# First attention of a four-layer kernel: constants loaded in order of use, later chunks' modulation and projections placed between heads

## The chip, the cores and the metric

The kernel runs on one core of a Trainium2 chip. The metric is the device time of one launch in microseconds (us), median of three runs. The core has five engines with a queue each, which work in the order of their queues and meet through semaphores: TensorE (PE; its weight loads are listed apart as PEld), VectorE (DVE), ScalarE (ACT), GpSimd (POOL) and SyncE (SP), which issues the loads here.

## What is computed

`x` has 16 samples of 128 tokens with 128 features, `cond_8` has 8 numbers a sample. Four layers follow, each `x = x + attention(condition(x))` and `x = x + ffn(condition2(x))`. The change touches the condition and the attention of layer 0 and the weights of its condition2:

```
# L0 condition: a linear layer plus low-rank parts, weighted by cond_8
y = x @ W_base.T + b_base + 2 * sum_e cond_8[:, e] * ((x @ As[e].T) @ Bs[e].T)
# L0 attention: 16 heads of 8 features; q, k and v are scaled by the cosine and the
# sine of a learned phase times an amplitude; softmax; output projection Wo
x = x + attention(y)
# L0 condition2: each sample has its own weight, a blend of 8 masked matrices
y = x @ (sum_g cond_8[:, g] * (weight[g] * mask)).T + bias
# L0 ffn: weights rounded to 4 bits in blocks of 32, activations to 16 bits with one
# scale for the whole tensor (a maximum over everything), so nothing passes it early
# layers 1 to 3: route tokens or samples by the two largest of 8 (top 2 of cond_8)
```

All tensors are 32-bit floats. The sample-wise weights come from `cond_8` alone, and so do the two largest experts of each sample (M8, IDX, WW), which the layers behind use.

## The kernel before

A program in Python writes one list, `order`, of steps (kind and operands); then each engine walks the same list and issues its own part of each step. So the order of the list is the order in every queue. `in_order` (line 64) makes the list from items: an item is a list of stages. In each round it takes one new item and does one stage of it and one stage of each item still alive, the newest first. Semaphore waits stand ahead of the instruction that needs them, and everything later in that queue waits too. Buffers come from rings: `take` gives the next free slot with the signals it must wait for, `give` returns it. For products there are four PSUM banks in ring RA, two in RB and two in RC.

The 16 samples are four chunks (n = 0 to 3) of four, 512 columns. The parts at issue:

- *Loads* (L1398, SP's queue): `cst` (the constants of the first stage, 844.5 KB), `x` in four parts of 256 KB, `l0b` (second projection weights), `w8` (eight matrices), `cst2`, `b2`, `fw` (ffn weights), `l1c`. TensorE and VectorE wait for `cst` and `x` before their first work, ScalarE and POOL for `cst`.
- *Modulation* of a chunk (`cond_items`, line 260): VectorE scales the low-rank matrices (L1995), TensorE multiplies (L1456), VectorE adds the base weight (L1999), TensorE applies the result to x (L1463), ScalarE evicts into Y (L1780). Chunk 0 is done at once, with `prep2` inside: the angle of the phases in six VectorE steps (L2002 to L1976), Sin on ScalarE (L1773), MOD (L2014), then the maxima (L2018) and indices (L2022) of cond_8 for later layers, and their mix with an Exp (L1775). Chunks 1 to 3 are items ahead of the attention.
- *Projection* of a chunk (`proj` in `mh_attn`): TensorE makes q and k with two products each (L1474, L1475) and v with four (L1482). VectorE shifts Y for v (L2041, L2042), turns q and k (stt, L1979) and spreads v (L2055).
- *Heads*: a chunk has 8 items ("heads" here, each one of 4 samples and one half of the 16 heads): scores (L1499), maxima and subtraction (L2075, L2078), exponent (L1792, L1795), turns (L1433, L1434 and the evictions L1800), values and sums (L1515, L1519), for the second half also the normalisation (L2085, L2087), at the end of a chunk the output product (L1526) and the sum into X (L2090). For each j of the four samples POOL makes masked copies of k (`kb`, L2551, four instructions of 128x256), one half item ahead.
- *Beside the heads*: from the fourth entry of the list on each takes up to two small steps: 33 of `wbot_steps` (the mask, L2094, then 4 x 8 blends: VectorE does one sample of four, L2100 or L1979, POOL the other three, each by a multiply (L2561) and an add (L2566)) and 20 of `ffn_weights` (L2109 to L2121, and turns L1531). Behind the last head stands `cond2` (L1540), which reads the blended weights.

Items run in this order: modulation of chunks 1 to 3, projection 0, projection 1, the heads of chunk 0, and projection n+1 in the middle of the heads of chunk n.

Of the kernel before, what the change touches and what calls it, by code (L numbers as in the profile page):

```python
# [15 lines left out]
NB = 16  # L16
S = 128
NC = 4
# [72 lines left out]
CONST = [("ident", 128), ("condT", 16), ("hm4", 4), ("mask", 128), ("sumw", 128),  # L91
# [11 lines left out]
CF = CL["maskT"][0]  # L103
# [34 lines left out]
def build(nc, xT, cst, l0b, w8, b2, fw, fd, l1c, moe1, l1f, moe2, moe3, l2f, moe4, l3f, xs, ys, out):  # L138
    with ExitStack() as ctx:
# [72 lines left out]
        def step(kind, **at):  # L212
# [13 lines left out]
            "cst": [(CC[:, 0:CF], cst[:, 0:CF])], "l0b": [(A1[:, 256:512], l0b)], "x": XIN, "w8": [(A0[:, 12800:13824], w8)],  # L226
# [16 lines left out]
        for name in ("cst", "x", "l0b", "w8", "cst2", "b2", "fw", "l1c"):  # L243
            load(name)
# [15 lines left out]
        def cond_items(key, i, src_key):  # L260
            items = []
            for n in range(NC):
                st = {}

                def s0(n=n, st=st):
                    at = step("cw", i=i, n=n, g=SG.take())
                    at["scaled"] = tick("cond_vec")
                    at["pa"] = RA.take()
                    at["mm"] = tick("cond_mm")
                    SG.give(at["g"], at["mm"])  # L270
                    at["w"] = st["w"] = SG.take()
                    at["sum"] = st["sum"] = tick("cond_vec")
                    RA.give(at["pa"], at["sum"])

# [11 lines left out]
        def mh_attn(i, in_key, out_key):  # L286
# [23 lines left out]
            for n in range(NC):  # L310
                st = chunk[n] = {}

                def proj(n=n, st=st):
                    if n == 0:
                        at = step("zeros", aps=[s.ap for s in RV.slots], after=[] if i == 0 else [sig["l2f_last"]])
# [3 lines left out]
                    if i == 0:  # L319
                        at["shift"] = tick("att_vec")  # L320
                    for x in "qk":
                        at["p" + x], at["r" + x] = RA.take(), RB.take()
                        at["mm" + x] = tick("att_mm")
                        if i == 3:
                            at["rot" + x] = tick("att_vec")
# [5 lines left out]
                    RY.give(at["y"], at["mmv"] if i == 0 else at["tk"])  # L331
                    at["tv"] = st["tv"] = tick("att_vec" if i == 0 else "att_act")
# [4 lines left out]
                items.append(([(in_key, n)], [proj] + [lambda: make_kb(0, 0)] * (n == 0), (out_key, "proj", n)))  # L337
# [98 lines left out]
            out_items = items[0:2]  # L436
# [10 lines left out]
        cond0[0][1][0]()  # L447
        at = step("prep2")
# [2268 lines left out]
```

## Time and profile before

| | us |
|---|---|
| median of three runs | 1411.71 (1410.06 to 1417.38) |
| the profiled execution | 1414.87 |
| its span | 1413.1 |
| TensorE busy in the span | 1240.8 (88%) |
| VectorE busy | 861.6 (61%) |
| ScalarE busy | 676.4 (48%) |
| POOL busy | 291.1 (21%) |

The profile is of one execution. Busy shares are means over stages with different limits. The stage at issue ends at 182.2 us of the span, where the first maxima of the ffn behind it stand.

### The profile page before, as it was taken

How to read it: one execution, taken by the hardware profiler on the slowest of the kernel's cores; microseconds unless marked ns; L12 is line 12 of the kernel's file. 1: busy time of each engine (PE TensorE's matmuls, PEld its weight loads, DVE VectorE, ACT ScalarE, POOL GpSimd, SP SyncE). 2: the span in 40 equal slices, each digit the busy share in tenths (PEclk: the TensorE clock that was granted, in tenths of full speed). 3: DMA queues.
4: the chain of work that ended last, by engine and by line, in shares of the span. 5: the costliest groups of instructions: out<-in, count | busy, mean ns of one | idle time of the engine just before them, and what ended most of it. 6: DMA issues, size and time to landing. Idle time of an engine off the chain costs nothing.

```text
span 1413.1 us, 26412 instructions
## 1 busy us (share of the span) xinstructions
PE 1240.8 (88%) x9301; PEld 962.8 (68%) x9301; DVE 861.6 (61%) x1828; ACT 676.4 (48%) x1358; POOL 291.1 (21%) x502
## 2 busy tenths in 40 slices
PE   4889970488999889999888999899999998898989
PEld 2455630156888889887777888498889754556877
DVE  3878668755456566656677565566554566664242
ACT  1556758545443334444444444244444375665553
POOL 1799400120002233330000013034310111100000
PEclk9999995699999999999999999999999999999999
DMA  8000010041050313104006001032020000000000
GB/s 310 1 2 2 2 75 0 32 169 61 1 202 26 108 45 101 48 25 178 28 1 266 37 7 48 25 107 75 29 90 2 1 2 1 1 1 1 0 15 16
DMA packets 42606, 75.71 MB, mean 54 GB/s; under 512 B 3816, under 2 KB 33520, under 8 KB 41584
## 3 DMA queue, kind: packets, MB, share of 16 engines
q1 hardware_dynamic: 38384, 65.62, 12.7%
q0 software_dynamic: 4096, 8.40, 1.9%
q8 instruction: 80, 1.31, 0.4%
q14 instruction: 46, 0.38, 0.1%
HBM read 59.72 MB, written 14.29 MB: 52 GB/s over the span
## 4 chain that ended last, share of the span: by engine, by line
PE 69%; DVE 15%; ACT 7%; issue 5%; POOL 2%; DVEq 1%; DMA 1%; SPq 0%; ACTq 0%; POOLq 0%
PE bank L1655 7%; PE bank L1644 7%; PE bank L1640 6%; PE bank L1699 5%; PE bank L1631 3%; PE bank L1433 3%; PE bank L1709 3%; PE bank L1499 3%; PE bank L1438 2%; PE bank L1440 2%; PE bank L1439 2%; PE bank L1624 2%; PE bank L1626 2%; PE bank L1625 2%; PE bank L1549 2%
## 5 line engine op out<-in xcount | busy, mean ns | idle before, releaser
L1892 ACT ACTIVATE SC<-bank 128x512 f32<-128x512 f32 x192 | 114.4, 596 | 217.9 <-PE bank L1640 123.2
L1979 DVE SCALAR_TENSOR_TENSOR SC<-bank,SM,SC 128x512 f32<-128x512 f32 x128 | 95.8, 749 | 124.9 <-PE bank L1644 108.2
L1655 PE MATMUL bank<-A,SC 128*128 x1024 | 136.9, 277 | 7.2 <-DVE SC L1979 6.2
L1644 PE MATMUL bank<-X,SC 128*128 128x128 f32 x1024 | 136.6, 276 | 6.1 <-DVE SC L2258 5.6
L1640 PE MATMUL bank<-X,SC 128*128 128x128 f32 x1024 | 135.6, 275 | 3.0 <-ACT SC L1876 2.8
L1640 PEld LDWEIGHTS bank<-X,SC 128*128 128x128 f32 x1024 | 126.2, 192 | 16.2 <-issue 10.2
L1655 PEld LDWEIGHTS bank<-A,SC 128*128 128x128 f32 x1024 | 125.5, 192 | 16.5 <-issue 15.6
L1644 PEld LDWEIGHTS bank<-X,SC 128*128 128x128 f32 x1024 | 124.5, 192 | 8.5 <-DVE SC L2258 8.4
L1699 PE MATMUL bank<-A 128*128 128x128 f32 x736 | 101.1, 281 | 11.1 <-DVE A L2408 5.6
L1792 ACT ACTIVATE A<-bank,SM 128x128 f32<-128x128 f32 x256 | 73.8, 383 | 66.2 <-DVE SM L2075 65.9
L1699 PEld LDWEIGHTS bank<-A 128*128 128x128 f32 x736 | 91.0, 195 | 15.7 <-ACT A L1917 8.7
L2551 POOL TENSOR_SCALAR A<-A,CC 128x256 f32<-128x256 f32 (+1 forms) x128 | 53.8, 439 | 209.2 <-DVE A L2069 109.4
L1876 ACT ACTIVATE SC<-A 128x512 f32 x128 | 80.6, 630 | 33.3 <-PE bank L1644 28.0
L2606 POOL DMA_INDIRECT A<-ys,POSI x64 | 62.1, 970 | 136.1 <-PE bank L1693 59.0
L2594 POOL DMA_INDIRECT xs<-CC,POSI x64 | 64.1, 1001 | 117.5 <-DVE POSI L2387 29.6
L2075 DVE TENSOR_REDUCE SM<-bank 128x4 f32<-128x512 f32 x128 | 81.9, 680 | 9.7 <-PE bank L1499 8.3
L1499 PE MATMUL bank<-A 64*128 64x512 f32 (+1 forms) x256 | 76.9, 677 | 10.9 <-POOL A L2551 4.7
L2238 DVE TENSOR_TENSOR SC<-bank,SC 128x512 f32<-128x512 f32 x64 | 44.2, 691 | 65.5 <-PE bank L1626 53.4
L1433 PEld LDWEIGHTS bank<-CC,A 128*128 128x128 f32 x408 | 47.7, 145 | 50.3 <-ACT A L1800 13.7
L1709 PE MATMUL bank<-BW,A 128*128 x552 | 77.5, 277 | 0.0
L1438 PE MATMUL bank<-R 128*128 128x512 f32 x176 | 69.4, 394 | 7.6 <-DVE SC L1979 6.0
L2577 POOL TENSOR_TENSOR SM<-SM 128x32 f32<-128x32 f32 x32 | 8.3, 258 | 316.3 <-DVE SM L1979 314.4
(322 smaller groups left out, 2613.5 us busy)
## 6 DMA issues: line engine op xcount, KB each, us to landing
A<-in_moe SPq DMA_DIRECT2D x36, 768.0 KB, 10.3
A<-xs SPq DMA_DIRECT2D x20, 256.0 KB, 3.4
ys<-A SPq DMA_DIRECT2D x20, 256.0 KB, 2.5
BW<-in_l1f SPq DMA_DIRECT2D x2, 2048.0 KB, 7.4
BW<-in_l2f SPq DMA_DIRECT2D x1, 3456.0 KB, 12.2
BW<-in_l1c SPq DMA_DIRECT2D x1, 3072.0 KB, 17.6
BW<-in_l3f SPq DMA_DIRECT2D x1, 2816.0 KB, 9.4
A<-in_l1c SPq DMA_DIRECT2D x1, 2560.0 KB, 8.7
```

Of the source, the lines that this page charges most:

```text
L1433: e.transpose(o[:, cut(r)], i[:, cut(r)], ident)
L1438: e.matmul(o, wh, hi, start=start, stop=False)
L1499: m = e.matmul(pa.ap, q[rows, a:a + 128], kb[rows, b:b + 512], start=at["i"] == 0, stop=True)
L1640: m = e.matmul(at["pg"].ap[:, cut(q)], wx[:, cut(q)], x, start=True, stop=True)
L1644: m = e.matmul(at["pu"].ap[:, cut(q)], wx[:, cut(4 + q)], x, start=True, stop=True)
L1655: m = e.matmul(o, at["h"].ap[:, cut(q)], W[:, bass.ds(r + (1024 + 128 * q), 128)], start=k == 0 and q == 0, stop=k == 1 and q == 3)
L1699: m = e.matmul(at["pa"].ap[:, cut(q)], at["wt"].ap[:, cut(q)], at["x"].ap, start=True, stop=True)
L1709: m = e.matmul(o, at["ht"].ap[:, cut(q)], BW[:, bass.ds(r + (dn + 128 * q), 128)], start=q == 0, stop=q == nk - 1)
L1876: e.activation(at["wx"].ap[0][:, 0:512], MOE_AT[at["L"]][:, bass.ds(r, 512)], ACT.Identity).then_inc(at["g"][0], 1)
L1892: e.activation(at["h"].ap, at["pg"].ap, ACT.Gelu_apprx_tanh).then_inc(at["gelu"][0], 1)
L1979: return e.scalar_tensor_tensor(out=o, in0=a, scalar=s, in1=b, op0=o1, op1=o2)
L2075: e.tensor_reduce(m[:, 4 * x:4 * x + 4], v4(pa.ap), AX, ALU.max, negate=True).then_inc(at["max"][x][0], 1)
```

## The change

The constants are put in order of use and loaded in parts: `c0` (what the first modulation needs, 205 KB), `x0`, `c1` (the rest of the first stage in two parts, 791 KB together; maskT and o0 are among them now), `l0b`, `w8`, `x1`, `cst2`, `x2`, `x3`, `b2`, `fw`, `l1c`. Engines wait for `c0` first, for `c1` and each `x` part where they use them; POOL waits for nothing at the start.

Modulation of chunk 0 is cut into scale, product, add and apply, with the angle behind the scale. The maxima, indices and mix become five steps (`route_steps`). Modulation and projection of chunks 1 to 3 become six items each chunk (scale; product and add; apply; q; k; v) between the heads of the chunk before; the second product of q and k takes a bank of RA in place of RB. The last attention keeps its order. Beside each head stands one blend step, and from the fourth head on one of the 25 other small steps. On POOL a blend step is one multiply and one add over three samples at once (128x384) where it was three of each (128x128).

```diff
-CONST = [("ident", 128), ("condT", 16), ("hm4", 4), ("mask", 128), ("sumw", 128),
+CONST = [("ident", 128), ("hm4", 4), ("mask", 128), ("sumw", 128), ("condT", 16),
...
-CF = CL["maskT"][0]
+C0, C1, CF = CL["condT"][0], CL["cond"][0], CL["c2b"][0]
...
-            "cst": [(CC[:, 0:CF], cst[:, 0:CF])], "l0b": [(A1[:, 256:512], l0b)], "x": XIN, "w8": [(A0[:, 12800:13824], w8)],
+            "c0": [(CC[:, C0:C1], cst[:, C0:C1])], "c1": [(CC[:, C1:CF], cst[:, C1:CF]), (CC[:, 0:C0], cst[:, 0:C0])],
+            "x0": XIN[0:1], "x1": XIN[1:2], "x2": XIN[2:3], "x3": XIN[3:4],
+            "l0b": [(A1[:, 256:512], l0b)], "w8": [(A0[:, 12800:13824], w8)],
...
-        for name in ("cst", "x", "l0b", "w8", "cst2", "b2", "fw", "l1c"):
+        for name in ("c0", "x0", "c1", "l0b", "w8", "x1", "cst2", "x2", "x3", "b2", "fw", "l1c"):
...
-                def s0(n=n, st=st):
-                    at = step("cw", i=i, n=n, g=SG.take())
+                def scale(n=n, st=st):
+                    at = step("cw_scale", i=i, n=n, g=SG.take())
                     at["scaled"] = tick("cond_vec")
-                    at["pa"] = RA.take()
+                    st["g"], st["scaled"] = at["g"], at["scaled"]
+
+                def product(st=st):
+                    at = step("cw", i=i, g=st["g"], scaled=st["scaled"], pa=RA.take())
                     at["mm"] = tick("cond_mm")
                     SG.give(at["g"], at["mm"])
-                    at["w"] = st["w"] = SG.take()
+                    st["pa"], st["mm"] = at["pa"], at["mm"]
+
+                def add(st=st):
+                    at = step("cw_add", i=i, w=SG.take(), pa=st["pa"], mm=st["mm"])
                     at["sum"] = st["sum"] = tick("cond_vec")
+                    st["w"] = at["w"]
                     RA.give(at["pa"], at["sum"])
+
+                def all3(scale=scale, product=product, add=add):
+                    scale()
+                    product()
+                    add()
 
                 def s1(n=n, st=st):
...
-                items.append(([(src_key, n)] if src_key else [], [s0, s1], (key, n)))
+                if src_key:
+                    items.append(([(src_key, n)], [all3, s1], (key, n)))
+                else:
+                    items.append([([], [scale], None), ([], [product, add], None), ([], [s1], (key, n))])
...
+                def shift(n=n, st=st):
+                    at = step("v_shift", n=n, y_in=sig[in_key, n], y=RY.take())
+                    at["t"] = tick("att_vec")
+                    st["y"], st["shift"] = at["y"], at["t"]
+
+                def q_k(x, n=n, st=st, shift=shift):
+                    u = {}
+
+                    def mm(x=x, n=n, st=st, u=u):
+                        if n == 0 and x == "q":
+                            at = step("zeros", aps=[s.ap for s in RV.slots], after=[])
+                            at["t"] = sig["zeros"] = tick("zeros")
+                        at = step("qk", n=n, x=x, y_in=sig[in_key, n], p=RA.take(), r=RA.take())
+                        at["mm"] = tick("att_mm")
+                        u.update(p=at["p"], r=at["r"], mm=at["mm"])
+
+                    def turned(x=x, st=st, u=u, shift=shift):
+                        at = step("qk_mod", x=x, p=u["p"], r=u["r"], mm=u["mm"], dst=(RQ if x == "q" else RK).take())
+                        at["t"] = st["t" + x] = tick("att_vec")
+                        RA.give(at["p"], at["t"])
+                        RA.give(at["r"], at["t"])
+                        st[x] = at["dst"]
+                        if x == "q":
+                            shift()
+
+                    return [mm, turned]
+
+                def v_parts(n=n, st=st):
+                    u = {}
+
+                    def mm(n=n, st=st, u=u):
+                        at = step("v", n=n, y=st["y"], shift=st["shift"], p=RA.take())
+                        at["mm"] = sig["Yfree", n] = tick("att_mm")
+                        RY.give(at["y"], at["mm"])
+                        u.update(p=at["p"], mm=at["mm"])
+
+                    def spread_out(st=st, u=u):
+                        at = step("v_out", p=u["p"], mm=u["mm"], zeros=sig["zeros"], v=RV.take())
+                        at["t"] = st["tv"] = tick("att_vec")
+                        RA.give(at["p"], at["t"])
+                        st["v"] = at["v"]
+
+                    return [mm, spread_out]
...
+                if i == 0:
+                    items.append([([(in_key, n)], q_k("q"), None),
+                                  ([(in_key, n)], q_k("k") + [lambda: make_kb(0, 0)] * (n == 0), None),
+                                  ([(in_key, n)], v_parts(), (out_key, "proj", n))])
...
+            out_items = list(items[0])
             for n in range(NC):
-                out_items += heads[8 * n:8 * n + 4]
-                if 1 <= n < NC - 1:
-                    out_items.append(items[n + 1])
-                out_items += heads[8 * n + 4:8 * n + 8]
+                hd = heads[8 * n:8 * n + 8]
+                if n == NC - 1:
+                    out_items += hd
+                else:
+                    q, k, v = ([x] for x in items[n + 1])
+                    scale, product, out = ([x] for x in before[n + 1])
...
-        cond0[0][1][0]()
-        at = step("prep2")
-        at["m"] = [tick("prep_dve") for _ in range(7)]
-        at["sin"] = tick("prep_sin")
-        t_mod = tick("mod")
-        at["r"] = [tick("prep_dve") for _ in range(2)]
-        at["exp"] = tick("prep_exp")
-        at["q"] = [tick("prep_dve") for _ in range(4)]
-        at["idx"] = t_idx = tick("idx")
-        t_ww = tick("ww")
-        cond0[0][1][1]()
+        scale, (product, add), last = (it[1] if len(it[1]) > 1 else it[1][0] for it in cond0[0])
+        scale()
+        at = step("angle")
+        at["m"] = [tick("prep_dve") for _ in range(6)]
+        at["sin"] = t_sin = tick("prep_sin")
+        product()
+        add()
+        at = step("mod", sin=t_sin)
+        at["m"], t_mod = tick("prep_dve"), tick("mod")
+        last()
         done.add(("y0", 0))
-        items = cond0[1:]
-        attn = mh_attn(0, "y0", "x0")
+        attn = mh_attn(0, "y0", "x0", cond0)
+        t_idx, t_ww = (S_("idx"), 1), (S_("ww"), 1)
+
...
+                        at["part"] = sig["wb3", b] = sig["wbot_pool"] = tick("wbot_pool")
+                        if g:
+                            at["acc"] = sig["wb3", b] = sig["wbot_pool"] = tick("wbot_pool")
+                            RWB.give(at["tmp"], at["acc"])
...
+        wb, fs, rt = wbot_steps(), ffn_weights(), route_steps()
+        beside_heads = [wb[0:1]] + [[w] for w in wb[1:]]
+        for k, f in enumerate(fs + rt):
+            beside_heads[3 + k].append(f)
         for k, it in enumerate(attn):
...
-            if k >= 3 and len(it[1]) > 1:
-                extra = [steps.pop(0) for _ in range(min(2, len(steps)))]
+            if it[0] == [("x0", "proj", 0)] or it[0] == [("x0", "proj", 1)] or it[0] == [("x0", "proj", 2)] or it[0] == [("x0", "proj", 3)]:
+                extra = beside_heads.pop(0) if beside_heads else []
+                if len(beside_heads) == 1 and it is attn[-1]:
+                    extra = extra + beside_heads.pop(0)
                 f0 = it[1][0]
...
-            w.wait_ge(*loaded["cst"])
-            w.wait_ge(*loaded["x"])
+            w.wait_ge(*loaded["c0"])
...
-                    if at["x"]:
-                        w.wait_ge(*at["x"])
+                    w.wait_ge(*(at["x"] or loaded[f"x{at['n']}"]))
...
-                    g = at["g"]
+                    b, g = at["b"], at["g"]
+                    to = WBOT[:, b + 1:b + 4, :]
+                    yb = COND.rearrange("p (b g) -> p b g", g=8)[:, b + 1:b + 4, g]
+                    part = at["tmp"].ap.rearrange("p (b o) -> p b o", b=3) if g else to
                     w.wait_ge(*at["mask"])
-                    for x in range(3):
-                        b = at["b"] + 1 + x
-                        tmp = A1[:, cut((x + 1) % 2)] if g else WBOT[:, b, :]
-                        if at["free"][x]:
-                            w.wait_ge(*at["free"][x])
-                        e.tensor_scalar(tmp, W8[:, g, :], COND[:, 8 * b + g:8 * b + g + 1], 1.0, ALU.mult,
-                                        ALU.mult).then_inc(at["tmp"][x][0], 1)
-                        if g:
-                            w.wait_ge(*at["tmp"][x])
-                            w.wait_ge(*at["prev_pool"][x])
-                            e.tensor_tensor(WBOT[:, b, :], WBOT[:, b, :], tmp, ALU.add).then_inc(at["acc"][x][0], 1)
+                    if g:
+                        over(at["tmp"])
+                    e.tensor_tensor(part, bc_mid(W8[:, g, :], 3), bc_last(yb, 128), ALU.mult).then_inc(at["part"][0], 1)
+                    if g:
+                        w.wait_ge(*at["part"])
+                        w.wait_ge(*at["prev_pool"])
+                        e.tensor_tensor(to, to, part, ALU.add).then_inc(at["acc"][0], 1)
...
```

The rest gives the steps their new names in each engine's walk: `cw` becomes `cw_scale`, `cw` and `cw_add`; `prep2` becomes `angle`, `mod`, `top_max`, `top_index` (eight samples each), `top_exp` and `top_mix`; `proj` of layer 0 becomes `v_shift`, `qk`, `qk_mod`, `v` and `v_out`, each with the instructions it had.

## Rows read from the trace of the kernel before

**Rows 1.** Stage table: start and end, length, busy of each engine (instructions), clock, DMA.

```profile
0.00:44.30 44.30, 23.42 (x72) 13.62 (x72) 19.55 (x89) 5.73 (x8) 8.77 (x16) 1.00 0.69 248
44.30:75.00 30.70, 22.87 (x227) 12.88 (x228) 26.64 (x51) 19.39 (x52) 25.82 (x60) 0.85 0.01 2
...
97.60:129.70 32.10, 31.68 (x376) 19.08 (x376) 28.25 (x55) 21.77 (x59) 29.62 (x70) 1.00 0.01 2
...
160.20:182.20 22.00, 19.65 (x278) 14.19 (x278) 13.87 (x26) 13.38 (x34) 0.00 (x0) 1.00 0.01 2
44.30:182.20 137.90, 124.32 (x1490) 76.42 (x1489) 110.69 (x209) 87.77 (x231) 102.29 (x236) 0.95 0.01 2
```

Busy columns are PE, PEld, DVE, ACT and POOL.

**Rows 2.** Chain of waits, 0 to 60 us: start, length, what it went through.

```profile
2.59 6.52 DMA X<-in_xT
...
13.34 0.15 DVE SC L2002
...
18.33 2.27 DVE IDX L2022 x17
...
39.15 0.89 PE bank L1463 x8
...
46.95 1.16 POOL A L2561 x3
48.10 1.95 POOL A L2551 x4
```

**Rows 3.** Chain of waits, 40 to 340 us.

```profile
74.30 2.08 PE bank L1499 x4
...
91.19 0.86 PE bank L1474 x2
...
109.04 1.06 PE bank L1499 x4
...
115.23 1.06 PE bank L1499 x4
```

**Rows 4.** Stage table, 45 to 55 us.

```profile
45.00:50.00 5.00, 1.92 (x9) 0.72 (x8) 4.93 (x12) 1.60 (x5) 3.06 (x7) 0.86 0.00 0
50.00:55.00 5.00, 5.00 (x16) 2.22 (x14) 4.81 (x10) 3.66 (x12) 4.49 (x12) 0.50 0.01 3
```

**Rows 5.** Instructions in order of time, 0 to 42 us: start, length, engine, line.

```profile
10.56 2.04 PE L1456 MATMUL bank<-SC,CC 128*128 128x512 f32 x2 [10.56 <-DVE SC L1995]
...
15.01 1.28 ACT L1773 ACT_TABLE_LOAD   x1 [15.01 <-DVE SC L1976]
...
33.55 0.68 DVE L2041 TENSOR_TENSOR A<-Y 128x508 f32<-128x508 f32 x1
...
35.52 1.02 PE L1475 MATMUL bank<-Y,A 128*128 128x512 f32 x2
...
40.42 0.86 DVE L2041 TENSOR_TENSOR A<-Y 128x508 f32<-128x508 f32 x1
```

**Rows 6.** DMA issues, 0 to 45 us: KB each, median us to landing.

```profile
CC<-in_cst SPq DMA_DIRECT2D x1, 844.5 KB, 4.4
```

**Rows 7.** POOL's groups by form, whole span: busy us, mean ns, idle before.

```profile
L2566 POOL TENSOR_TENSOR A<-A 128x128 f32<-128x128 f32 x84 | 39.6, 471 | 7.0
L2561 POOL TENSOR_SCALAR A<-A,CC 128x128 f32<-128x128 f32 x96 | 37.9, 398 | 4.5 <-DVE A L2094 3.1
L2551 POOL TENSOR_SCALAR A<-A,CC 128x256 f32<-128x256 f32 x64 | 30.7, 497 | 30.1 <-DVE A L1979 30.1
...
L2586 POOL TENSOR_TENSOR A<-A 128x512 f32<-128x512 f32 x3 | 3.8, 1265 | 12.5 <-DVE A L2167 12.5
```

**Rows 8.** VectorE's line L1979, 44.3 to 350 us: ns least, median, most.

```profile
L1979 DVE SCALAR_TENSOR_TENSOR A<-A,CC x28: 340/352/601, 48.9 to 149.9; 128x128 f32<-128x128 f32 x28
...
L1979 DVE SCALAR_TENSOR_TENSOR A<-bank,SM,CC x9: 740/743/752, 44.2 to 125.8; 128x512 f32<-128x512 f32 x9
```

**Rows 9.** VectorE's groups by form, 44.3 to 182.2 us.

```profile
L1979 DVE SCALAR_TENSOR_TENSOR A<-A,CC 128x128 f32<-128x128 f32 x28 | 11.8, 421 | 0.2
```

More of the change, by code:

```diff
@@ L313, in proj @@
                 def proj(n=n, st=st):
                     if n == 0:
-                        at = step("zeros", aps=[s.ap for s in RV.slots], after=[] if i == 0 else [sig["l2f_last"]])
+                        at = step("zeros", aps=[s.ap for s in RV.slots], after=[sig["l2f_last"]])
                         at["t"] = sig["zeros"] = tick("zeros")
@@ L435, in mh_attn @@
                         heads.append(([(out_key, "proj", n)], stages, gives))
-            out_items = items[0:2]
-            for n in range(NC):
-                out_items += heads[8 * n:8 * n + 4]
-                if 1 <= n < NC - 1:
-                    out_items.append(items[n + 1])
-                out_items += heads[8 * n + 4:8 * n + 8]
+            if i == 3:
+                out_items = items[0:2]
+                for n in range(NC):
+                    out_items += heads[8 * n:8 * n + 4]
+                    if 1 <= n < NC - 1:
+                        out_items.append(items[n + 1])
+                    out_items += heads[8 * n + 4:8 * n + 8]
+                return out_items
@@ L442, in mh_attn @@
+            out_items = list(items[0])
+            for n in range(NC):
+                hd = heads[8 * n:8 * n + 8]
+                if n == NC - 1:
+                    out_items += hd
+                else:
+                    q, k, v = ([x] for x in items[n + 1])
+                    scale, product, out = ([x] for x in before[n + 1])
+                    out_items += (hd[0:1] + scale + hd[1:2] + product + hd[2:3] + out + q + hd[3:4] + k + hd[4:5] + v + hd[5:8])
             return out_items
@@ new lines, in build, with route_steps, top, index @@
+        t_idx, t_ww = (S_("idx"), 1), (S_("ww"), 1)
+        def route_steps():
+            u = {}
+            def top():
+                at = step("top_max")
+                at["t"] = u["max"] = tick("prep_dve")
+            def index(k):
+                at = step("top_index", k=k, max=u["max"])
+                if k == 1:
+                    at["t"] = tick("idx")
+            def weigh():
+                at = step("top_exp", max=u["max"])
+                at["d"], at["exp"] = tick("prep_dve"), tick("prep_exp")
+                u["exp"] = at["exp"]
+            def mixed():
+                at = step("top_mix", exp=u["exp"])
+                at["q"] = [tick("prep_dve") for _ in range(4)]
+                at["t"] = tick("ww")
+            return [top, lambda: index(0), lambda: index(1), weigh, mixed]
@@ L464, in build @@
         WBOT = A1[:, 8192:10240].rearrange("p (b o) -> p b o", b=16)
+        RWB = Ring([A1[:, 10240 + 384 * k:10624 + 384 * k] for k in range(2)])
         WUG = BW[:, 6144:6912].rearrange("p (n o) -> p n o", o=128)
@@ L2035, in _ @@
                     w.wait_ge(*q[3])
-                    stt(WW, W0, 1.0 / 12, W1, ALU.mult, ALU.add).then_inc(t_ww[0], 1)
-                elif kind == "proj" and at["i"] == 0:
+                    stt(WW, W0, 1.0 / 12, W1, ALU.mult, ALU.add).then_inc(at["t"][0], 1)
+                elif kind == "v_shift":
                     y4, Yc = v4(at["y"].ap), ch(Y, at["n"])
@@ L2069, in _ @@
                         e.tensor_tensor(at[x].ap, at[x].ap, at["y"].ap, ALU.add).then_inc(at["t" + x][0], 1)
+                elif kind == "v_out":
+                    over(at["v"])
+                    w.wait_ge(*at["mm"])
+                    w.wait_ge(*at["zeros"])
+                    for j in range(4):
+                        i = e.tensor_tensor(vtiles(at["v"].ap, j), heads_of(at["p"].ap[:, cut(j)]), heads_of(MODV), ALU.mult)
+                    i.then_inc(at["t"][0], 1)
                 elif kind == "rowmax":
```

135 lines of the change are left out of this document (66 added, 69 removed).

## The prediction

> **What bounds the kernel now.** I read the stage table first [rows 1]. The run's own time was 1414.87 us for a span of 1413.1, 1.8 us outside it; the median of the three runs is 1411.71 (1410.06 to 1417.38), so the sum below is made on 1414.87 and its gain is then taken off the median. The change touches the first 182 us: the prologue (to 44.3, where the first scores of the first attention start) and that attention with the modulation behind it (44.3 to 182.2). In the prologue TensorE is busy 23.4 of 44.3 us and VectorE 19.6: nobody is full, it is a chain. In the attention TensorE is busy 124.3 of 137.9, VectorE 110.7, POOL 102.3. All that follows starts from a maximum over the whole stream, so each microsecond saved before 182.2 should be saved at the end: nothing behind it has a date of its own, since the loads issued at the start are in long before 182.
>
> The chain of waits [rows 2] shows the prologue's parts: 6.5 us for x to land before VectorE does anything, and at 46.95 and 48.10 the chain goes over to POOL, which works on the blended weights (L2561, L2566) and the masked keys (L2551) in turn (pieces of 0.36 and 0.45 and the keys again) until TensorE takes it back at 74.3 [rows 3]. From there on it is mostly TensorE: the scores of every second head start 6.19 us apart (109.04 to 115.23), so a head costs 3.1 us, and between 97.6 and 129.7 TensorE is busy 31.7 of 32.1 us.
>
> The clock matters too. [...] It also shows in durations of the prologue [rows 5]: the first product (128x512, two pieces) takes 2.04 us at 10.56; the same size takes 1.02 at 35.52, behind eight microseconds of nearly unbroken work, and moves on by 0.86 in the chain [rows 3]. So cold products cost 2.04, warm ones 0.86.
>
> **Before, as a sum.** Warm work of TensorE in 44.3 to 182.2: 16 pairs of heads x 6.19 = 99.0; 4 output products 3.4; the projections of two chunks, each four products of 0.86 and one group of eight pieces like the 0.89 of [rows 2], 4.5 x 2 = 9.0 (that of chunk 1 lies before 44.3); four modulation groups of 0.9, 3.6; nine weight transposes, 2. Together 117. [...]
>
> **The change, part by part.**
>
> *Order of the loads.* One issue more (0.4 us of SP, hidden: x lands long after its issue). VectorE now waits for c0 alone, 401 columns or 205 KB, where it waited for 844.5 KB and 1024 KB of x. The big piece took 4.4 us from issue to landing [rows 6], at 5.1; a part of 205 KB lies between 1.8 (all of the 4.4 in proportion) and 5.1; I take 3.4. c1 ends 1252 KB into the queue, between 844 KB at 5.1 and 1868 KB at 9.1: 6.7, say 7.0. So the first VectorE work moves from 9.2 to 3.4, and the six steps of the angle, which ran from 13.3 [rows 2] to the table load at 15.0 [rows 5], to 7.0.
>
> *What is left of the prologue.* Scale 0.7, product 2.04 cold: done at 6.6, hidden behind c1. Angle 1.8 (7.0 to 8.8), weight sum 0.7 to 9.5, modulation group 2.1 to 11.6; Sin's table load 1.28 and Sin lie beside that [rows 5]. Eviction 0.7 to 12.3. Then q (two products, 4.1 cold) to 16.4, and k: 1.7 warm, 4.1 cold. VectorE needs 1.4 for q (two like those of 0.74 in [rows 8]), 0.85 for the shift, 1.4 for k, and POOL four masked copies of 0.5, 2.0 [rows 7]: first scores at 22.1 if the clock rises in time, 23.9 if not. I take 23, against 44.3: 21.3 us earlier. Gone from that path: the maxima and index searches (2.3 us the latter [rows 2]), Exp's table, three chunks of modulation, one projection.
>
> *What comes back between the heads.* TensorE: three modulations at 0.86 + 0.89 = 1.75, 5.3, and the projection of chunk 1, 4.5. Its warm work becomes 117 + 9.8 = 127. VectorE: 2.9 of the projection, 3 x 1.3, and 5.1 for the maxima (1.1), indices (2.3 [rows 2]) and the mix and copies (an estimate, 1.7): 110.7 + 11.9, less 1.9 of maxima that belong behind the stage: 121. Exp's table load (1.28) now stands in the first head; it is in the filling below.
>
> *POOL.* Before, one step is three samples, each a multiply (0.398) and an add (0.471) and 0.07 between, 2.7 us, and up to two steps a head. Now it is one multiply and one add of 128x384. No row has that size or a stretched operand: the nearest are 0.471 at 128 and 1.265 at 512 columns [rows 7], which bound it, and in proportion it is 1.0; so 2.1 a step, one step a head. With half of four masked copies of 0.5 a head costs POOL 3.1, as much as TensorE, and the masked copies are asked for before the step in each head. The stretch 50 to 75, in which TensorE waited for POOL, should go. All of it is 60 x 1.0 + 31 = 91, hidden under 127. What is late next is TensorE itself.
>
> *Waits that the items add.* The six items of a chunk are single stages. Behind `product` on TensorE stand turns and values of older heads; it waits for a scale that VectorE did two slots before. `q` waits for Y, which ScalarE evicts while TensorE does the values of an older head (1.4 against 0.7). Two banks of the ring of four are held by q or k where RB's were used, so the scores behind them wait until VectorE has turned them; VectorE has about 9 us of work against TensorE's 10 between q and the third scores after it. I put 1.5 us a chunk on these, between 0 and 4, 4.5 in all. The last blending steps sit on the last head, and the modulation behind reads them: POOL may run up to three heads ahead (ring of three masked keys), 9 us, against 10.7 for its last five steps: 0 to 2 us, taken as nothing.
>
> *Sum.* Work 127; filling of the first heads 5 (before: 1.9 of work in 45 to 50 and Exp's table on top); one cold stretch 3.4; waits of the items 4.5; drain 2.4 as in the last stage of [rows 1]: 142. 23 + 142 = 165 against 182.2: 17 us. 1411.7 - 17 = **1394.5 us**.
>
> [...] The shift of two SBUF operands took 0.68 at 33.55 with POOL idle and 0.86 in its place at 40.42 with POOL at the masked copies [rows 5]; the blend on VectorE (two SBUF operands as well) is 0.340 at least, 0.601 at most [rows 8], its mean beside POOL's 0.37 to 0.47 us instructions 0.421 [rows 9]. So about 0.08 is waited each time. With POOL instructions of 1.0 it should be 0.2: on the forty or so such operations some 5 us more of VectorE, 126 in 142. That is in the sum as slack, not as a term. [...]
>
> **Rivals.**
> - *VectorE becomes the bound* (20%). 121 of work and 5 of waits, and it is stopped itself in order (products, transposed values). Between 44.3 and 75 it was busy 26.6 of 30.7, 87%: 126 / 0.87 = 145, with fill and drain of 6: 23 + 151 = 174: 8 us, 1403. For it: in chunk 0 it has some 33 us of work against TensorE's 32. Against: 28.3 of 32.1 did not hold TensorE in [rows 1].
> - *More than I forecast* (17%): clock up at once, no item waits: 22 + 127 + 8 = 157: 25 us, 1387.
> - *Slower* (5%): POOL's long instructions lock VectorE out. Place: the blends, shifts, scales and weight operations in the attention, forty. It decides from where VectorE's sum passes 182.2 - 23 - 6 = 153, i.e. 27 us more than 126, a whole 0.7 to 0.8 us on each. [...]
> - *The change doesn't do what it says* (3%): the time saved is given back behind 182 by another phase of the clock or of the queues; 1411. For it: the clock's low level came and went with TensorE's pauses in [rows 4], and those shift. Against: the work behind is the same in the same order.
> - Forecast: 55%.
>
> **Numbers.** Forecast's own range is 1389 to 1401 (items 0 to 12 us in all, first scores 22 to 24, run to run 3). For 8 in 10 I go from 1385 to 1405, which takes in the middle of both neighbours. What can be told from no change is 0.5%, 7 us. Faster by more than that: forecast and its better neighbour 0.72, and two thirds of the VectorE case: 0.85. Same 0.10. Slower 0.05.
>
> **What would show it.** First VectorE instruction near 3.4 us; angle at 7; first scores at 22 to 24; POOL's blend near 1.0 us; no run of POOL in the chain between the first scores and 60; pairs of heads 6.2 apart late in each chunk; maxima of the next stage at about 165 where they stood at 182; from there on distances as before. I am wrong if POOL's instructions are much over 1.3, if VectorE's blends average over 0.7, or if the gain at the maxima is not found at the end.

## The result and the profile after

The changed kernel takes 1408.22 us in the median of 20 runs (1399.98 to 1409.9), the kernel before 1411.21; ratio 0.9965, 95% interval 0.9951 to 0.9978. The gain is small but clear of the noise: 3.0 us between the medians, 5 by the ratio. I had forecast 17 and a range that began 6 us down; the measured time lies above its end of 1405. One execution of the kernel before, of 1885 us at a mean granted clock of 0.64, is left out of every ratio and fit below.

The profiled execution of the changed kernel has a span of 1403.5 us. Its stage table, columns as in [rows 1]; the last row answers to 44.30 to 182.20 there, the others are cut at the output product of each chunk:

```profile
0.00:24.70 24.70, 10.53 (x28) 5.39 (x28) 11.46 (x23) 3.56 (x4) 8.19 (x13) 0.98 0.91 345
24.70:72.60 47.90, 42.94 (x428) 25.18 (x429) 38.21 (x69) 27.39 (x71) 36.15 (x52) 0.90 0.18 52
72.60:107.50 34.90, 33.21 (x388) 20.33 (x387) 30.68 (x58) 23.07 (x59) 21.77 (x31) 1.00 0.00 1
107.50:149.60 42.10, 36.80 (x446) 22.32 (x444) 39.03 (x117) 26.23 (x71) 26.50 (x37) 1.00 0.01 2
149.60:172.40 22.80, 19.64 (x278) 14.20 (x278) 15.77 (x31) 13.93 (x35) 0.00 (x0) 1.00 0.01 2
24.70:172.40 147.70, 132.59 (x1535) 82.03 (x1535) 123.69 (x274) 90.62 (x234) 84.42 (x120) 0.97 0.06 18
```

The first scores start 19.6 us sooner, but from there to the end of the stage it takes 147.7 us where it took 137.9: half of the lead is given back. The third chunk (107.5 to 149.6) is the slow one: 42.1 us where the chunk before it took 34.9. Half of these 7.2 us is work (TensorE busy 36.8 against 33.2), the other half TensorE standing still (5.3 against 1.7). The same table for a stretch of that chunk shows who was full, VectorE with 24.55 of 25 us, while TensorE stood for 4.2:

```profile
120.00:145.00 25.00, 20.80 (x277) 12.81 (x275) 24.55 (x91) 16.79 (x48) 24.29 (x34) 1.00 0.01 2
```

The chain of waits there runs through VectorE's maxima of the scores (L2189) with the moved maxima (L2126), indices (L2131) and mix (L2142) between them, and the stage ends at 172.4, where the idle stretch begins:

```profile
126.41 0.75 DVE SM L2126 x10
127.17 1.19 DVE SM L2189 x2
129.61 0.75 DVE IDX L2131 x6
130.36 1.19 DVE SM L2189 x2
133.29 0.76 DVE IDX L2131 x6
134.04 1.19 DVE SM L2189 x2
...
139.65 0.91 DVE SM L2142
...
142.39 1.27 DVE SM L2189 x2
...
172.41 4.17 issue
```

The prologue in order of time (start, length, engine, line):

```profile
1.67 3.55 POOL L2654 MEMSET A<- 128x2048 f32 x2
3.30 1.95 DVE L2092 TENSOR_SCALAR SM<-CC 128x16 f32<-128x16 f32 x1 [3.30 <-DMA CC<-in_cst]
8.76 0.23 DVE L2106 TENSOR_SCALAR SC<-CC 128x130 f32<-128x130 f32 x1 [2.78 <-DMA CC<-in_cst]
17.61 1.41 DVE L2084 SCALAR_TENSOR_TENSOR A<-bank,SM,CC 128x512 f32<-128x512 f32 x2 [4.90 <-PE bank L1569]
24.68 3.78 PE L1603 MATMUL bank<-A 64*128 64x512 f32 x8 [3.71 <-POOL A L2664]
```

VectorE starts at 3.3. The angle starts at 8.8. Before the first q is there VectorE sits idle for 4.9 us; the maxima, indices and mix, which now stand where it is full, would nearly fit in there.

POOL's groups, 0 to 200 us, answering to [rows 7], and VectorE's blend, 24.7 to 172.4 us, answering to [rows 9]:

```profile
L2664 POOL TENSOR_SCALAR A<-A,CC 128x256 f32<-128x256 f32 x64 | 33.1, 537 | 50.8 <-DVE A L2084 28.1 <-PE bank L1531 13.1 <-PE bank L1603 9.6
L2678 POOL TENSOR_TENSOR A<-A 128x384 f32<-128x384 f32 x28 | 29.4, 1051 | 2.2
L2674 POOL TENSOR_TENSOR A<-A,CC 128x384 f32<-128x384 f32 x32 | 26.9, 840 | 0.0
```

```profile
L2084 DVE SCALAR_TENSOR_TENSOR A<-A,CC 128x128 f32<-128x128 f32 x28 | 13.6, 485 | 0.0
```

### The profile page after: what moved, and what is told of

Same layout as the page of the kernel before. It is cut to its first block, busy times and chain, and to the rows that moved or that the text cites. A ratio compares the mean times of both kernels' runs of the same rounds, so it can differ in the third digit from the quotient of the medians.

```text
span 1403.5 us, 26293 instructions
## 1 busy us (share of the span) xinstructions
PE 1236.4 (88%) x9301; PEld 960.1 (68%) x9301; DVE 866.8 (62%) x1828; ACT 677.1 (48%) x1358; POOL 273.2 (19%) x382
## 3 DMA queue, kind: packets, MB, share of 16 engines
q8 instruction: 80, 1.31, 0.4%
## 4 chain that ended last, share of the span: by engine, by line
PE 69%; DVE 16%; ACT 8%; issue 5%; DVEq 1%; DMA 1%; POOL 0%; ACTq 0%; SPq 0%; POOLq 0%
PE bank L1759 7%; PE bank L1748 7%; PE bank L1744 6%; PE bank L1803 5%; PE bank L1735 3%; PE bank L1530 3%; PE bank L1813 3%; PE bank L1603 3%; PE bank L1535 3%; DVE SM L2189 2%; PE bank L1537 2%; PE bank L1536 2%; PE bank L1728 2%; PE bank L1730 2%; PE bank L1729 2%
## 5 line engine op out<-in xcount | busy, mean ns | idle before, releaser
L2189 DVE TENSOR_REDUCE SM<-bank 128x4 f32<-128x512 f32 x128 | 81.8, 679 | 9.7 <-PE bank L1603 9.7
L1813 PE MATMUL bank<-BW,A 128*128 x552 | 77.5, 277 | 0.0
L1530 PE MATMUL bank<-CC,A 128*128 128x128 f32 x408 | 69.2, 287 | 4.1 <-DVE A L2084 1.4
```

The source lines that it names most:

```text
L1530: e.transpose(o[:, cut(r)], i[:, cut(r)], ident)
L1813: m = e.matmul(o, at["ht"].ap[:, cut(q)], BW[:, bass.ds(r + (dn + 128 * q), 128)], start=q == 0, stop=q == nk - 1)
L2189: e.tensor_reduce(m[:, 4 * x:4 * x + 4], v4(pa.ap), AX, ALU.max, negate=True).then_inc(at["max"][x][0], 1)
```

## The experiments

"Stage end" is the start of the idle stretch behind the last modulation in the chain of waits, 182.15 in the kernel before. It is read from one trace each and repeats within 1 to 3 us; ratios are against the kernel before on the same chip. "Busy" and "idle" are TensorE's, between the first scores and the stage end. For the same work busy grows with the time spent at the lower clock (129.8 us at a mean clock of 0.99 in the last but one row, 134.3 at 0.96 in the second trace of the changed kernel), while idle is what TensorE waited for the others. In all, V says that VectorE's work held the stage, P that its waits beside POOL's instructions did, T that TensorE's clock ate the gain. V and P can both hold.

| kernel | first scores | stage end | busy | idle | ratio (95% interval) |
|---|---|---|---|---|---|
| before, two traces | 44.3, 44.8 | 182.2, 182.6 | 124.3, 124.4 | 13.5, 13.4 | |
| changed, three traces | 24.7, 24.9, 25.4 | 172.4, 173.7, 175.0 | 132.6, 134.3, 134.2 | 15.1, 14.6, 15.3 | 0.9965 (0.9951 to 0.9978), 0.9937 (0.9914 to 0.9959), 0.9965 (0.9951 to 0.9980) |
| narrow blends, two traces | 24.7, 24.9 | 169.0, 168.6 | 132.6, 131.5 | 11.7, 12.2 | 0.9888 (0.9867 to 0.9909), 0.9916 (0.9898 to 0.9934) |
| maxima early | 25.3 | 169.2 | 132.4 | 11.5 | 0.9908 (0.9884 to 0.9933) |
| narrow, maxima early | 25.4 | 168.2 | 131.8 | 11.1 | 0.9918 (0.9901 to 0.9936) |
| narrow, items ahead | 38.6 | 171.9 | 118.8 | 14.5 | 0.9939 (0.9924 to 0.9954) |
| narrow, old pace | 24.9 | 167.4 | 130.2 | 12.3 | 0.9920 (0.9904 to 0.9936) |
| narrow, ahead, old pace | 41.0 | 183.1 | 123.5 | 18.5 | 0.9998 (0.9983 to 1.0014) |
| the same, maxima early (loads and prologue alone) | 39.2 | 181.3 | 122.2 | 19.9 | 0.9998 (0.9987 to 1.0010) |
| narrow, old pace, maxima early | 24.1 | 166.7 | 130.0 | 12.6 | 0.9895 (0.9874 to 0.9916) |
| all blends on POOL | 24.8 | 165.6 | 130.4 | 10.4 | 0.9902 (0.9878 to 0.9927) |
| all on POOL, maxima early | 25.1 | 165.1 | 129.8 | 10.1 | 0.9893 (0.9878 to 0.9908) |
| before, wide blends | 42.3 | 179.9 | 122.3 | 15.2 | 0.9996 (0.9980 to 1.0012) |

**Maxima, indices and mix early.**

```diff
+        for f in route_steps():          # right behind MOD in the prologue
+            f()
-        wb, fs, rt = wbot_steps(), ffn_weights(), route_steps()
+        wb, fs, rt = wbot_steps(), ffn_weights(), []
```

> The changed kernel, but the maxima, indices, exponent and mix stand in the prologue, right behind MOD, where VectorE sat idle for 4.9 us before the first q product was there; nothing of them stands beside the heads. Theory V (VectorE is the bound where these steps stood, 120 to 145 us of the changed kernel's trace): the stage's end moves from 172.4 to 167, the median falls by 4 to 6 us below the changed kernel's. [...] Theory T (what the stage gains is eaten by TensorE's clock in other places): the stage's end moves, the median does not.

169.2 against a mean of 173.7: 4.5 us. 3.5 of them are TensorE's idle time (11.5 against 15.0). The rest is busy time in the third chunk, where two of the three traces of the changed kernel had a stretch at half clock and this one had none. VectorE's busy time in the stretch fell by 5.3 us (123.7 to 118.4). The gain stands where theory V wants it: the third chunk took 38.7 us, where the three traces of the changed kernel have 42.1, 43.6 and 44.4, and the chunk before it took 35.0 in all four. Theory V holds; under theory P alone I had put 0 to 2 us on this edit. The median fell by 4.5 us on one chip (1405.3 to 1400.7), and the first scores moved by 0.6 us at most.

**Narrow blends.** The changed kernel with three multiplies and three adds of 128x128 a step on POOL, as before.

```diff
-                    e.tensor_tensor(part, bc_mid(W8[:, g, :], 3), bc_last(yb, 128), ALU.mult).then_inc(at["part"][0], 1)
...
+                    for x in range(3):   # with its waits and its add, as in the kernel before
+                        e.tensor_scalar(tmp, W8[:, g, :], COND[:, 8 * b + g:8 * b + g + 1], 1.0, ALU.mult, ALU.mult)
...
```

> The changed kernel with the blends on POOL as they were, three pairs of 128 columns a step instead of one pair of 384. [...] Theory V: VectorE gets back some 3 us of waits, but POOL needs 2.7 us a step against 1.95, 3.7 us a head with the keys against TensorE's 3.1, so the stage ends 5 to 20 us later, and POOL stands in the chain of waits.

POOL needs more time for it (77.5 us of blends where it had 56.3) and the stage still ends 4.9 us sooner (168.8 in the mean of two traces). 3.0 us of that are TensorE's idle time (12.0 against 15.0), the rest its clock. VectorE's blends fell to 0.408 us, its four multiplies (L2213 of the changed kernel) from 0.671 to 0.328. Theory P, for which I had put the blends at 0.42 and the stage end 3 to 6 us sooner, holds; my own case that POOL would bind is refuted. Row of VectorE's blend, 24 to 172 us:

```profile
L2086 DVE SCALAR_TENSOR_TENSOR A<-A,CC 128x128 f32<-128x128 f32 x28 | 11.4, 408 | 0.0
```

> The changed kernel with narrow blends again, beside the changed kernel itself on the same chip. The stage ends 3.4 to 4.7 us sooner. If what comes behind is the same but for the spread of the clock, the difference of the medians, taken at equal mean clock, is 3 to 5 us; if the wide form also costs behind the stage, 8.

At the mean clock of its runs (0.9705) and of the changed kernel's (0.9665) the two lie 1400.6 and 1407.4 on one chip; 4 to 5 of the 6.8 us go with the clock, by the slope found below. So at equal clock it is 2, less than I expected; the stage ends say 6.4 on this chip. But on the first chip too the narrow kernel had the higher clock (0.9710 against 0.9672, 6.8 us between the means), so the clock may be a part of what the edit does, and taking it out may take out too much. With six runs on each chip this isn't settled.

**Wide blends alone**, in the kernel before.

> The kernel before with one edit, the blends on POOL in the new wide form, still up to two steps a head. If POOL was the bound between 46 and 75 us there, a step falls from 2.7 to 2.0 us and the eleven or so steps that stand in that stretch give 5 to 8 us: median 1404 to 1406, which would be as much as the whole change. [...]

The median does not move. The stage ends 2.3 us sooner, but 2.0 of these stand ahead of the first scores (42.3), before POOL's first blend. Behind them TensorE's clock gave 2.0 back (busy 122.3 against 124.3) and it stood idle for 1.7 more. So the wide form brought nothing here: not the 5 to 8 us of a POOL that is the bound. VectorE's blends rise to 0.700 us, where POOL has up to two steps a head and is busy 29.3 of the 32.7 us from 42.3 to 75; they were 0.421 in [rows 9]:

```profile
L1977 DVE SCALAR_TENSOR_TENSOR A<-A,CC 128x128 f32<-128x128 f32 x28 | 19.6, 700 | 0.2
```

**VectorE and POOL by themselves.** PHASES gives, one after the other, VectorE's form and POOL's.

```diff
+        PHASES = [("two", None, 0, 0), ("two", "tt", 128, 12), ("two", "tt", 256, 8), ("two", "tt", 384, 6), ...
+                        m = e.scalar_tensor_tensor(out=o, in0=a, scalar=IN[:, 256:257], in1=b, op0=ALU.mult, op1=ALU.add)
+                        m = e.tensor_tensor(o, a, b, ALU.add)      # POOL, w columns
```

> A kernel by itself that leaves the whole computation out: sixteen VectorE operations of 128x128 with two SBUF operands, alone and beside POOL adds of 128, 256, 384 and 512 columns and beside POOL multiplies by a column; then VectorE with one PSUM operand, and a tensor_scalar, beside POOL adds of 384; POOL alone. [...]

By theory P I had estimated 0.4 to 0.5 us for VectorE's operation beside adds of 128 columns, about 1.0 beside 384 and 1.3 beside 512, and no slowing of the one with a PSUM operand. The rival was a slowing by one factor, the same at 128 and at 512 columns.

VectorE's operation alone and beside adds of 128, 256, 384 and 512 columns (ns least, median, most; one row from a window each):

```profile
L171 DVE SCALAR_TENSOR_TENSOR DO<-IN x16: 347/348/352, 6.2 to 10.2; 128x128 f32<-128x128 f32 x16
...
L171 DVE SCALAR_TENSOR_TENSOR DO<-IN x13: 352/536/543, 10.6 to 15.9; 128x128 f32<-128x128 f32 x13
...
L171 DVE SCALAR_TENSOR_TENSOR DO<-IN x9: 352/806/812, 17.2 to 22.6; 128x128 f32<-128x128 f32 x9
...
L171 DVE SCALAR_TENSOR_TENSOR DO<-IN x7: 352/1076/1080, 25.3 to 30.6; 128x128 f32<-128x128 f32 x7
...
L171 DVE SCALAR_TENSOR_TENSOR DO<-IN x6: 352/1344/1351, 34.0 to 39.4; 128x128 f32<-128x128 f32 x6
```

At all four lengths one VectorE operation passed for each POOL instruction, after one at the start: 13 for 12 adds, then 9 for 8, 7 for 6 and 6 for 5. Each 128 columns more on POOL add 0.27 us. That is the waiting of theory P and not a slowing by one factor. It is VectorE that pays: POOL's add of 128 columns took 0.452 us alone and 0.497 beside VectorE, that of 384 0.991 and 1.036, 0.045 more each and not a whole VectorE operation. Beside POOL's multiplies by a column (0.399) VectorE's operation took 0.452. Of the other forms, groups by form over the whole run:

```profile
L175 DVE TENSOR_SCALAR DO<-IN 128x128 f32<-128x128 f32 x16 | 7.1, 520 | 2.7 <-POOL PO L195 2.7
...
L173 DVE TENSOR_TENSOR DO<-PS,IN 128x128 f32<-128x128 f32 x16 | 3.3, 282 | 0.0
```

With one operand from PSUM no wait shows beside adds of 384 columns (0.280 to 0.291, the normalisation's 0.292 in the attention), and sixteen took 3.3 us. The tensor_scalar from SBUF shows waits: its first took 1.04 us, half of them took 0.216 or less.

**What the interleaving and the pace are worth.** Three kernels with narrow blends.

```diff
+            for n in range(1, NC):       # items ahead: modulation of a chunk as one item
+                (_, (scale,), _), (_, (product, add), _), (_, (out,), key) = before[n]
+                out_items.append(([], [lambda s=scale, p=product, a=add: (s(), p(), a()), out], key))
+            out_items += items[1]        # and projection n+1 in the middle of chunk n
...
+        beside_heads = [steps[2 * k:2 * k + 2] for k in range((len(steps) + 1) // 2)]   # old pace
```

> Narrow blends on POOL, and the modulation of chunks 1 to 3 and the projection of chunk 1 back ahead of the first head, those of chunks 2 and 3 whole in the middle of the chunk before; loads, prologue, pace and the route steps beside the heads stay. Theory: three modulations and a projection cost 17 to 19 us ahead of the heads (half of it on the cold clock) and give back 9.8 us of TensorE's work and the waits of the items between the heads: first scores at 40 to 43, stage end at 173 to 177, median 1402 to 1407. If the interleaving brought nothing, 169 and 1397.

> Narrow blends on POOL, and the small steps two a head again from the first head on, in the old mix, instead of one blend a head. Theory: POOL then has 6.4 us of work a head in the first four heads, it holds the masked keys back as in the kernel before, and the chain of waits runs over POOL for 20 to 25 us: stage end 175 to 180. If the pace did not matter, 169.

> Narrow blends, and both things put back that each alone cost little: the items ahead of the heads (stage end 171.9 alone) and two small steps a head (167.4 alone), against 169.0 with neither. Theory R (each of the two by itself is enough to take POOL off the path, since items between the heads give POOL the time and one blend a head gives it less to do): together the stall on POOL after the first heads is back, the chain runs over L2676 and L2681 for 20 us or more, stage end 177 to 182, median 1405 to 1409. Rival (the two are independent): their effects add, 169.0 + 2.9 - 1.6 = 170.3.

Items ahead cost 3.1 us, not 4 to 8; the old pace cost nothing, against my 6 to 11 (its 1.4 us less are TensorE's clock, the idle time is 12.3 against 12.0); both together cost 14, with 18.5 of idle. Theory R holds. The chain of waits of the last one, beyond its first scores, is the one of [rows 2] again:

```profile
42.20 1.55 POOL A L2680 x4
...
48.84 1.88 POOL A L2670 x4
...
58.69 0.47 POOL A L2685
60.15 1.12 POOL A L2680
...
62.69 1.83 POOL A L2670 x4
64.65 2.08 PE bank L1609 x4
```

So each of the two edits takes the stall away by itself. On top of the interleaving the pace adds nothing; on top of the pace the interleaving adds the 3.1 us, which is hardly more than one trace differs from the next.

**The loads and the prologue alone.**

> The loads in order of use and the prologue that goes with them, the maxima in its idle time; items ahead of the heads, two small steps a head, narrow blends: the kernel before but for the prologue. First scores at 41 to 42 us against 44.3; what it gains there is 3 us, if the stall on POOL behind the first heads does not take it back. Stage end 178 to 181; median 1407 to 1411. If the order of the loads were the larger part of the change: under 175.

First scores 5 us sooner (I had expected 2 to 3), stage end 1.1 us sooner, median the same: the rest is waited for at POOL, where the chain of waits runs from 40.4 to 62.7 us.

**VectorE relieved.** No blend on VectorE (its whole step is taken out); POOL does four samples at once (128x512, 1.09 and 1.31 us).

```diff
-                    to = WBOT[:, b + 1:b + 4, :]
+                    to = WBOT[:, b:b + 4, :]
...
```

> The changed kernel with all four samples of a blend step on POOL (128x512) and none on VectorE. VectorE loses 28 blends and four multiplies, 16 us with their waits. POOL needs 2 x 1.3 a step and 1.0 of keys, 3.6 a head, 115 in all against a stretch of 148. [...] If POOL's own pace is the bound: later than 172. [...]

The earliest stage end so far, 8 us before the changed kernel's mean and inside the 162 to 167 that I had put for theories P and V together, with the longest POOL instructions of all and with POOL at 98 us. VectorE has 112.3 us in 24.8 to 165.6, where it had 123.7. Of the 8 us 4.6 are TensorE's idle time (10.4 against 15.0), most of it in the third chunk (2.3 against 5.3 to 6.1). The other 3.3 are its clock: 2.2 in the first chunk, where its mean lay between 0.89 and 0.97 in the traces, and 1.3 in the third.

> Both edits that helped, together: POOL's blends in three pairs of 128 columns, and the maxima, indices and mix in VectorE's idle time of the prologue. Separately they ended the stage at 169.0 and 169.2 us against 172.4 to 173.7. If they relieve the same engine (VectorE) in the same stretch, the second still helps as long as VectorE is full there: stage end 165 to 167, median 1394 to 1397. If the first has already made TensorE or POOL the bound, nothing is added: 169, 1397.

> The three edits with the earliest stage ends together: narrow blends, two small steps a head, and the maxima and indices in the prologue's idle time (VectorE then has 5.5 us less beside the heads). If VectorE is still full in any stretch: stage end 163 to 166, median 1394 to 1397. If TensorE is the bound everywhere by now, as the pair of 169.0 and 168.2 hints: 166 to 168, 1397 to 1401.

> All four samples of a blend on POOL (512 columns) and the maxima and indices in the prologue's idle time. Alone they ended the stage at 165.6 and 169.2 us against 172.4 to 173.7. If VectorE is still full where the maxima stood: 161 to 163, median 1392 to 1396. If TensorE's own work (127) with the filling has become the bound: 164 to 166, 1395 to 1400.

Once VectorE has room, more room brings 0 to 1 us each: 168.2, 166.7, 165.1, each the second branch of its expectation, nothing or little added. TensorE's idle time is 10.1 to 12.6 us in all kernels with VectorE relieved and interleaved items. The intervals of the three ratios overlap. None of the kernels is shown to beat narrow blends alone. All three ratios lie below the changed kernel's, though the intervals of the first two reach into the changed kernel's on one chip.

**The clock.**

> The changed kernel again, nothing edited, for a second trace and for the spread. Theory T: the half-clock stretches of TensorE fall elsewhere and are of another length, and the run's time goes with them: each 3.4 us more at half clock costs up to 1.7 us. The stage's end stands at 171 to 176. Otherwise the trace repeats within 1 us, 172.4, and the spread of the times comes from behind it.

> The changed kernel a third time. Theory T: its runs lie on one line of time against mean clock, 12 us for each 0.01 of clock, with the same line as in its twenty runs before; median 1403 to 1409 as the clock falls out, stage end at 172 to 174.

> The kernel before, nothing edited, for a second trace. Theory T (the first trace of it, an execution of 1414.87 against a median of 1411.2, had more half clock in the attention than most): stage end at 178 to 180 instead of 182.2, with one stretch of half clock there instead of two. Otherwise 182 again, and the difference of the medians is lost behind the stage.

The changed kernel's third stage end, 175.0, lies 1 us above what I expected. In two of the three traces the clock fell in the third chunk, where TensorE stood for VectorE. In the second trace it was 0.57 from 144 to 148 us, after TensorE had been busy for 1.9 of the 4 us before; in the third it was 0.73 from 144 to 148, with TensorE busy for 2.0 of these 4 us. TensorE's busy time in the chunk was 38.3 us in both, against 36.8 in the first trace. In all eight traces of kernels with VectorE relieved and the items interleaved, the chunk's mean clock was 1.00. So VectorE's stall likely costs some 1.5 us of clock as well, two times out of three; no run shows this by itself.

The stage end of the kernel before repeats, 182.6, and so do its half-clock stretches: I was wrong that its first trace was unusual there. Over 38 runs of the changed kernel the time goes with the mean granted clock (correlation -0.85, 12.5 us for 0.01), over 67 of the kernel before too (-0.83, 9.4 us). Fitted at 0.967 they give 1406.1 and 1413.3, 7.2 us apart; the plain means are 1406.8 and 1412.5, 5.6 apart, because the changed kernel's mean clock was 0.9664 and the other's 0.9679. A correlation does not say which of the two makes the other. The second half of the expectation on the traces held: what lies behind the stage took 1230.9 to 1233.3 us in both. In the traces, then, the whole gain arrives: the spans are 9.2 us apart in the mean. But the two traced executions of the kernel before (1414.9 and 1417.8 us) are slower ones than its mean.

## Why the prediction was wrong

- *Start of the first scores*: 23, measured 24.7 to 25.4. Right in kind, 2 us off. c0 landed where I said (3.3 for 3.4), but c1 let the angle start at 8.8, not 7.0. (The profile gives c0 200.5 KB where I have 205; I had counted thousands of bytes there, which moves my landing times by 0.1 us.) The first small VectorE operation took 1.95 us and ended with POOL's memset, a cost hidden here.
- *Cold and warm products*: I called those of 2.04 us in the prologue cold. The profile's granted clock reads 1.00 there (10 to 12.6 us, as from 35 to 42, where they take 1.02), so that they ran at half clock is inferred from the factor two and not recorded. Where the profile does record it, the factor is the same: four scores took 2.08 us at 49.65, where the clock reads 0.50 (it stays there to 55 [rows 4]), and 1.06 at 109.04, where it reads 1.00.
- *POOL's blend*: 1.0 and 2.1 a step, measured 0.84 and 1.05. Right.
- *The stall on POOL goes*: right. I had put it to the pace and the wide form; the crossed kernels show that either the pace or the interleaving does it, and the wide form isn't needed.
- *TensorE's work and the cold stretch*: 127 + 3.4, measured 132.6 to 134.3, so 2 to 4 us more. No run shows the term of 3.4. What the traces show instead: in the first, TensorE had half clock from 24.7 to 34.0 and was busy for 7.9 of these 9.3 us, which costs some 4; in the other two some of it lay in the third chunk, behind VectorE's stall (mean 0.96 where it was 1.00), in the second trace 0.50 from 25.0 to 28.4 and again from 144.5 to 147.9.
- *The step that failed* is the term for VectorE: "some 5 us more of VectorE, 126 in 142. That is in the sum as slack, not as a term." VectorE was busy 123.7 us, even less than that, but it is not spread evenly. I summed it over the whole stage and never asked over which heads the moved work lands. The program puts the maxima, indices and mix beside heads 24 to 28 of 32; in time they fell between 125 and 142, where VectorE came to 24.55 of 25. My sum leaves TensorE 12 us of idle time (filling 5, items 4.5, drain 2.4) and 1.5 for the third chunk; measured are 14.6 to 15.3, and 5.3 to 6.1 in the third chunk. The other chunks' idle time is near the sum's, 4.4 to 5.0, 1.7 and 3.1. Taking those steps out brought the whole down to 11.5, shortening what VectorE waits for beside POOL to 12.0, taking the blends off it to 10.4: what I had forecast.
- *So the sum's miss at the stage end*, 173.7 for 165, is 2 us of first scores, 3 of waiting for VectorE and some 3 of TensorE's clock. The waiting is what the experiments show. About 1 of the clock's 3 us stood in the third chunk and likely came with it.
- *The rivals*: "VectorE becomes the bound", 20%, had the stage end at 174; the three traces have 172.4, 173.7 and 175.0. Its mechanism is what happened, but that its number fits is partly luck, since the clock in the first chunk added its share. Its place was wrong: it named chunk 0. There VectorE was full too (19.7 of the 20 us from 45 to 65), but relieving it took only 0.8 us off that chunk's idle time.
- *VectorE's waits beside POOL*: I scaled an average of 0.08 us up to 0.2 by the length of POOL's instructions. In the traces the blend's time went with how much of the time POOL was in an instruction and with how long it was: 0.421 us with two steps of short instructions a head, 0.408 with one such step, 0.485 with one step of long ones, 0.700 with two of long ones. Beside POOL without a pause VectorE got one operation in for each POOL instruction (0.348 us alone, 1.344 beside 512 columns), while POOL lost 0.045 us an instruction.
- *From stage to end*: 8.7 us at the stage (means of two and three traces) became 5.6 in the means and 3.0 in the medians of the result. 1.6 of the difference goes with the mean clock by the fit. The clock's fall behind VectorE's stall is a likely reason for the changed kernel's lower clock; whether it is all of it stays open, and the share of half clock differs from run to run by more than that.

## What to carry to other kernels

When work is moved from an idle stretch into a full one, sum each engine over the few heads where it lands, not over the stage: 5 us of small VectorE steps cost 3.5 of TensorE's time there and nothing that can be told in the prologue's idle time, 100 us earlier. Here longer instructions saved POOL time (56.3 us of blends for 77.5) and VectorE paid (0.485 us a blend for 0.408, both operands from SBUF); look at whose time is short before fusing. Split a stage's length into TensorE's busy and idle time before calling a gain your edit's: here up to 4 us between traces of the same work were its clock. Where two edits both aim at one stall, try each without the other: here either alone was enough to take it away.

## What the runs showed of the hardware

A VectorE operation of 0.348 us with two SBUF operands took 1.344 beside POOL adds of 512 columns, while POOL's adds of 128 and 384 columns grew by 0.045 us beside it. A VectorE tensor_scalar of 16 columns took 1.95 us (3.30 to 5.25) beside memsets of 2048 columns on POOL, which ended at 5.22; in the kernel before it took 0.47 (9.22 to 9.69), and the memsets ended at 9.66. Each time it ended 0.03 us behind them. I had not expected that, and no run takes the memset away, so that it waited for them is not shown. The mean granted clock of the changed kernel's first twenty runs went from 0.963 to 0.972, and their times from 1409.5 to 1400.0 us with it.
